# The gate scores of a mixture-attention block: three 32-column products for each 96-column one

## The reference

```python
gates = jax.nn.softmax(x @ wg_w, axis=-1)
_, idx = jax.lax.top_k(gates, ROUTED)
mask = jax.nn.one_hot(idx, E_ROUTED, dtype=gates.dtype).sum(-2)
rg = gates * mask
denom = jnp.clip(rg.sum(-1, keepdims=True), jnp.finfo(rg.dtype).eps, None)
routed_gates = rg / denom * ROUTED
...
shared_gates = jax.nn.softmax(x @ wg1_w, axis=-1) * SHARED
w0 = jax.nn.softmax(x @ wg0_w, axis=-1) * 2.0
shared_gates = w0[..., 0:1] * shared_gates
routed_gates = w0[..., 1:2] * routed_gates
masked_gates = jnp.concatenate([shared_gates, routed_gates], axis=-1)
o = (masked_gates[..., None] * o).reshape(B, N, H * HD)
```

## Time and profile before

| | us |
|---|---|
| median of 3 runs | 570.95 |
| lowest and highest of them | 568.47, 573.49 |
| span of the profiled execution | 569.6 |
| TensorE matmul busy in it | 515.9 (91%) |
| TensorE weight load busy in it | 396.6 (70%) |
| VectorE busy in it | 406.6 (71%) |
| ScalarE busy in it | 299.0 (52%) |
| GpSimd busy in it | 97.0 (17%) |

### The profile page before, as it was taken

The page is one execution under the profiler, slowest core; times in us unless marked ns, Lnnn a source line. Parts: engine busy times, 40 slices in busy tenths (PEclk is TensorE's granted clock), DMA queues, the critical chain, the costliest instruction groups (busy, mean ns, idle before and its releaser), DMA issues.

```text
span 569.6 us, 11352 instructions
## 1 busy us (share of the span) xinstructions
PE 515.9 (91%) x4673; PEld 396.6 (70%) x4673; DVE 406.6 (71%) x891; ACT 299.0 (52%) x488; POOL 97.0 (17%) x85
## 2 busy tenths in 40 slices
PE   5799989898999999999999999999969798989696
PEld 5576667677887566786976667777945677686475
DVE  4234877688777957779768857869749688748982
ACT  0125446356338546858346546866335568525762
POOL 6022400100320422110010422100010231011200
PEclk9799999979999999999999999999998999999999
DMA  9995020000000000100000000000000000000000
GB/s 215 287 203 142 17 63 0 8 2 2 0 2 1 2 1 2 57 8 2 1 22 1 3 1 0 1 1 1 2 22 1 1 2 2 1 22 1 1 1 22
DMA packets 12675, 16.02 MB, mean 28 GB/s; under 512 B 6235, under 2 KB 10048, under 8 KB 12240
## 3 DMA queue, kind: packets, MB, share of 16 engines
q1 hardware_dynamic: 9712, 12.71, 9.4%
q10 hardware_dynamic: 2400, 2.00, 1.1%
q0 software_dynamic: 512, 0.59, 0.6%
HBM read 14.11 MB, written 1.18 MB: 27 GB/s over the span
## 4 chain that ended last, share of the span: by engine, by line
PE 70%; DVE 17%; ACT 7%; issue 3%; POOL 1%; DMA 1%; ACTq 0%; DVEq 0%; POOLq 0%
PE ps L692 16%; PE ps L1005 9%; PE ps L702 8%; PE ps L682 7%; PE ps L825 4%; PE ps L783 3%; DVE smax L1715 3%; DVE pr L1741 3%; PE ps L1066 2%; PE ps L1180 2%; DVE psum L1729 2%; PE ps L1202 2%; PE ps L1156 2%; PE ps L1056 2%; PE ps L840 2%
## 5 line engine op out<-in xcount | busy, mean ns | idle before, releaser
L1715 DVE TENSOR_REDUCE smax<-ps 96x12 f32<-96x1152 f32 (+1 forms) x28 | 37.8, 1351 | 18.1 <-PE ps L1056 10.8
L1729 DVE TENSOR_REDUCE psum<-pr 128x12 f32<-128x1152 f32 (+1 forms) x24 | 32.3, 1344 | 4.3 <-ACT pr L1371 4.3
L1366 ACT ACTIVATE pr<-ps,less 128x96 f32<-128x96 f32 (+1 forms) x96 | 24.6, 337 | 17.9 <-DVE less L1717 17.8
L1409 ACT ACTIVATE squares<-ps 128x1536 f32<-128x1536 f32 x12 | 17.4, 1450 | 27.5 <-PE ps L702 21.6
L1957 POOL TENSOR_TENSOR side_wide<-attn,w_mask 128x1024 f32<-128x1024 f32 (+1 forms) x12 | 20.7, 1748 | 59.1 <-ACT attn L1261 47.4
L1828 DVE TENSOR_REDUCE ss<-squares 128x24 f32<-128x1536 f32 x12 | 21.0, 1749 | 12.1 <-ACT squares L1409 12.1
L1983 POOL TENSOR_TENSOR squares<-squares,qk_root 128x512 f32<-128x512 f32 x8 | 16.7, 2082 | 75.0 <-DVE qk_root L1504 75.0
L1931 POOL TENSOR_TENSOR ln_root<-ln_root,minus_half 128x3 f32<-128x3 f32 x8 | 6.8, 856 | 129.5 <-DVE ln_root L1603 129.5
L682 PE MATMUL ps<-w_cqkv,side_c 64*96 64x384 f32 (+1 forms) x96 | 27.4, 500 | 0.0
L1005 PE MATMUL ps<-w_ff,b_kB 128*128 128x192 f32 x144 | 25.5, 329 | 0.0
L692 PE MATMUL ps<-w_cqkv,side_c 128*128 128x512 f32 (+1 forms) x72 | 25.0, 492 | 0.0
(11 more groups left out here) (360 smaller groups left out, 1356.8 us busy)
## 6 DMA issues: line engine op xcount, KB each, us to landing
x_in<-in_xT SPq DMA_DIRECT2D x3, 768.0 KB, 4.5
b_kB<-in_cqkv SPq DMA_DIRECT2D x1, 1152.0 KB
w_cqkv<-in_cqkv SPq DMA_DIRECT2D x1, 864.0 KB
out<-side_c ACTq DMA_DIRECT2D x3, 288.0 KB, 2.3
w_cqkv<-in_cqkv SPq DMA_DIRECT2D x1, 855.0 KB
heads<-in_xT ACTq DMA_DIRECT2D x3, 256.0 KB, 3.8
side_in<-in_patchT SPq DMA_DIRECT2D x3, 192.0 KB, 4.4
side_tok<-in_tok_ff SPq DMA_DIRECT2D x2, 288.0 KB, 6.9
```

What stands on the lines that cost most here:

```text
L1366: m = act.activation(e[:, s % 2, h * N:(h + 1) * N], t[0:rows, h // 4, h % 4 * N:(h % 4 + 1) * N], ACT.Exp, scale=head ** -0.5, bias=less[ ...
L1715: dve.tensor_reduce(mx, t, AX.X, ALU.max).then_inc(w.S[stage + "_sub"], 1)
L1729: dve.tensor_reduce(psum[0:rows, s % 2, :], e, AX.X, ALU.add).then_inc(w.S[done], 1)
```

## The change

Each product of 96 stationary columns becomes three products of 32 columns, which write partitions 0 to 31, 32 to 63 and 64 to 95 of the same 14 columns of the same bank. The index `n` runs over 12 products for each piece: `n % 3` is the block of 32 tokens, `n // 3` the sample. The list at the end names the column block as the "bank", so that the first product of each block, instead of the first of all, opens the accumulation, and the last of each closes it. The sums, the bank, the semaphore and the order of the units stay as they are.

```diff
                 k14 = EXPERTS + 4
-                split_product([t[0:N, s * k14:(s + 1) * k14] for s in range(GS)],
-                              lambda s, kc, r: w.y.cT[r, kc, s * N:(s + 1) * N],
-                              lambda s, kc, r: w_cgate[r, kc, :], fill_sem(w, ("c_g", 0)), narrow_first(w, ("c_g", 0)), (0,) * GS, [0] * GS)
+                split_product([t[n % 3 * 32:n % 3 * 32 + 32, n // 3 * k14:(n // 3 + 1) * k14] for n in range(3 * GS)],
+                              lambda n, kc, r: w.y.cT[r, kc, n * 32:(n + 1) * 32],
+                              lambda n, kc, r: w_cgate[r, kc, :], fill_sem(w, ("c_g", 0)), narrow_first(w, ("c_g", 0)),
+                              (0,) * 3 * GS, [0, 1, 2] * GS)
```

## The result

| | kernel before | changed kernel |
|---|---|---|
| median beside each other | 570.32 us (14 runs) | 567.95 us (14 runs) |
| ratio, 95% interval | | 0.9953, 0.9935 to 0.9971 |
| the same comparison later, on another set of runs | 571.43 us (23 runs) | 569.70 us (12 runs) |
| ratio, 95% interval | | 0.9968, 0.9937 to 0.9998 |
| span of the profiled execution | 569.6 us | 565.7 us |

The change makes the kernel faster by 0.3 to 0.5%. The time lies in the predicted range (567.2 to 573.4 us), but the medians differ by 2.4 us in the first comparison and by 1.7 us in the second, where the sum had 0.9 us and its best bound 1.1 us. A gain of 0.9 us is a ratio of 0.9984: outside the first interval, inside the second. So part of the gain may be a term that the sum did not have.

What follows compares the result with a forecast made beforehand. TensorE was taken to bound the run only where the chain passes through it. Savings of 0.35 us (third gate unit) and 0.54 us (fourth), -0.9 us on a median of 570.95 us, gave 570.1 us, range 567.2 to 573.4 us.

Steps and rivals of the forecast that it cites:

- the sum: Whole kernel: savings of 0.35 us at the third and 0.54 us at the fourth gate unit, -0.9 us.
- its best bound: Whole kernel: the largest gain by the bounds, -0.36 and -0.73 us at the third and fourth units, -1.1 us.
- Which units count: Four gate units: the first two gain 0 because VectorE is late; the third and fourth are on the chain.
- What a record costs in blocks: Gate products: three blocks of columns load at once, so a 32-column record costs 11 ns without an issue limit.
- the lower bound: Gate products without a limit on issue: 11 ns a record, 0.26 us a half unit, 0.53 us both halves.
- the second half: Second 24 records of a gate unit: taken at 0.46 us, the middle of 0.26 and 0.67 us.
- added changes of shape: Borders of gate units: 0.10 us each, two added at the third unit and one at the fourth.
- issue is the bound: Rival, gate products: a pair needs some 28 ns to issue in whatever blocks; +0.3 us, 571.2 us; chance 0.22.
- rule on drains: TensorE in gate units: changing the tiling mode drains it, another tile of the same mode does not; 0.10 us a drain.
- What is late next: Behind the third unit, transposes wait for `u`, cutting 0.44 to 0.35 us; behind the fourth nothing is late, 0.54 us.
- a rival on the slower side only: Gate units on the chain: thin work lowers TensorE's clock behind them, 3.5 us each, +7 us, 577.95 us; chance 0.03.
- The likeliest case's own range: Whole kernel: forecast gain of 0.4 to 1.1 us without the spread of runs, 569.8 to 570.6 us; chance 0.50.

Runs made afterwards that it cites:

- partner: The kernel before run once more with no edit, against itself; ratio 0.9998 (0.9969 to 1.0027).
- groups 2 and 3: Kernel before with blocks of 32 columns only in the third and fourth gate units; ratio 0.9970 (0.9942 to 0.9998) against the kernel before.
- group 3: Kernel before with blocks of 32 columns only in the fourth gate unit; ratio 0.9962 (0.9941 to 0.9982) against the kernel before.
- groups 0 and 1: Kernel before with blocks of 32 columns only in the first and second gate units; ratio 0.9998 (0.9974 to 1.0022) against the kernel before.
- dense dummies ahead: Kernel before with seven full-array dummy products ahead of the real ones in the third and fourth gate units; ratio 1.0214 (1.0175 to 1.0253).
- dummy in the wait: Kernel before with one full-array dummy product in TensorE's 0.84 us wait ahead of the fourth gate unit; ratio 0.9996 (0.9975 to 1.0017).

## Why the prediction was right, and where it was short

**Which units count.** Right. The first two give nothing (+0.1 +/- 0.2 us), for the reason named: VectorE takes up the scores as late as before, and TensorE's lead of 0.6 us becomes a wait of 0.90 us in place of 0.24. From the first gate unit to the third the changed kernel takes 451.73 - 183.85 = 267.88 us, and its partner with the same falls 451.59 - 183.73 = 267.86 us.

**What a record costs in blocks.** Right at the lower bound. The three blocks load side by side; a half of 24 records goes in 0.27 us and one change of shape, the price per record is 11 ns, and a change of shape is 0.10 us. The step that was mis-sized is the second half: I took 0.46 us, the middle between free issue and issue at 28 ns a pair, and it took 0.27. A unit takes 0.73 us to the next one's start, not 0.94. The added changes of shape cost what the sum had: the one ahead of the first unit shows as its start 0.12 us behind the partner's (183.85 and 183.73), while VectorE is only 0.03 us behind (184.59 and 184.56). The rival "issue is the bound", with 0.22, was given too much: of 240 records in a row, the first 239 came with no sign of it, though a run that long does stop once for 1.1 us. The Trainium skill's rule that stood beside that rival (TensorEngine Tiling (Array Packing), Instruction Overhead) gave an estimated 25 ns for each matmul; the trace has 11 ns, and the measurement decides. Its rule on drains (the same page, Key Properties) agrees with the trace: 0.10 us at each change of shape.

**What is late next.** The mechanism was right at the third unit, the size too large: 0.22 us gained, not 0.35. I had looked at the third tile of `u`, for the last transposes; the first ones already wait, and start 0.04 us after VectorE's second tile. At the fourth it was 0.72 us against 0.54, by about the 0.19 us of the mis-sized second half.

**The sum at an equal clock.** Forecast 0.9 us; 0.22 + 0.72 = 0.9 us by the traces, 1.2 +/- 0.2 us by the fit (0.8 us with a slope of 1). The last stretch says the same: from the start of the fourth unit to that of VectorE's last instruction it is 566.50 - 511.37 = 55.13 us before and 562.55 - 508.13 = 54.42 us after, both with the clock at 1.00 from one to the other. That the sum met the traces so well is in part luck: it had 0.13 us too much at the third unit and 0.18 us too little at the fourth.

**What the sum does not have: the clock.** Over all runs with a listed clock the changed kernel is 2.2 us faster in the mean (571.13 and 568.96), of which the fit gives 1.2 us to the shorter path and 1.0 us to the clock (0.0024 x 570 x 0.71); with a slope of 1 it is 0.8 and 1.4 us. I had the clock as a rival on the slower side only: that thinner work in blocks would make it fall more. In these runs it fell less. The rest of the first ratio, 0.9953 against 0.9962 over all runs, is within its interval.

Why it fell less is open. That a long stretch of thin products brings the clock down is shown by the two kernels with 12 us of thin and of dense products. That the single unit of the kernel before does so, and the shorter one does not, is not shown. For it: one profile (509.8 us) and the means. The three kernels with the fourth unit in blocks (changed, groups 2 and 3, group 3; 50 runs) have 0.9860 +/- 0.0005, the two with it in 96 columns (before, groups 0 and 1; 111 runs) 0.9841 +/- 0.0004, a difference of 0.0020 +/- 0.0006, or 0.8 us. Against it: the kernel with groups 2 and 3 taken alone has 0.9845, not above the others. And the traces bear it out weakly. Of the five with the fourth unit once in 96 columns (before, before once more, groups 0 and 1, dense dummies ahead, dummy in the wait) one has a fall behind it; of the seven with it once in blocks none has. One fall of 3.4 us takes 0.003 off the mean clock, so it would have to stand there in two runs of three. Elsewhere falls come and go more than that: seven of the fourteen traces have one at 112 or 113 us, ahead of every gate unit, three of them in kernels with blocks, and all but one of these falls are 6.8 us long, 0.006 of the mean clock. So chance, or something that the edit moves far from the gate units, stays a rival for the clock's 1.0 us.

**The range.** It held because the spread of single runs was put into it. The likeliest case's own range, 569.8 to 570.6 us, did not hold the time: it had the path and not the clock. That the time lay in the stated range is thus no proof of the whole account: the path's 0.9 us is borne out, the rest of the gain is not explained.

## What to carry to other kernels

A product of 96 stationary and 14 moving columns cost its weight load here, 85 ns a record from start to start. Cutting it into blocks of 32 columns, with a different block in each successive product, let three loads run side by side, 11 ns a record; the order was worth 0.6 us of the 0.75 us. Before counting such a gain, look at what is late next at each place, and then at the clock: a long stretch of thin products on a path that TensorE bounds costs time behind it too (9 us beside 12.2 us of work here), and a change of 1 us can't be read from two traces whose falls of the clock differ, since one fall is worth up to 1.7 or 3.4 us. Compare stretches of equal clock between fixed products instead: the fourth unit's gain is read from one pair of starts, to a few hundredths of a us.

## What the runs showed of the hardware that was not expected

- In a run of 80 records with 96 stationary and 14 moving columns, back to back, the granted clock went to 0.50, though in the 3.8 us up to that the matmuls were recorded as busy for all of it and the weight loads for 3.59 us; 12 us of full products ahead of one pass of 16 did not do it. A busy share near 100% in the profile does not tell that the clock will stay up.
- TensorE starts products of other column blocks ahead of the program's order, but only some: 48 records take 0.73 us with the blocks in turn and 1.32 us with eight records in a row on each, and there the second and third block begin three records ahead of their turn.
- A long run of 32-column records (15 ns each) stops for 1.1 and 1.3 us from start to start, 239 and 176 records in, at "issue". At 85 ns a record no such stop was seen in 80.
